# One 105-word row table per hop, a buffer for x, and hop 1's products with a PSUM operand, in a two-hop graph attention kernel

## The reference

```python
edge_index = jnp.stack([src, dst]); head, tail = edge_index
for _ in range(2):
    a_input = jnp.concatenate([ent[head], ent[tail]], axis=-1)
    e_input = jnp.sum((a_input @ fc_w.T + fc_b) * rel[etype], axis=-1)
    e = jax.nn.leaky_relu(e_input, negative_slope=0.2)
    m = jax.ops.segment_max(e, head, num_segments=n)
    exp_e = jnp.exp(e - m[head])
    alpha = exp_e / jax.ops.segment_sum(exp_e, head, num_segments=n)[head]
    ent = jax.ops.segment_sum(ent[tail] * alpha[:, None], head, num_segments=n) + ent
    ent = ent / jnp.maximum(jnp.linalg.norm(ent, axis=-1, keepdims=True), 1e-12)
out = layernorm(x + ent)
```

## Time and profile before

| | us |
|---|---|
| three runs | 2890.5, 2903.3, 2920.0 (median 2903.3) |
| the profiled execution, its own time | 2912.7 |
| its span | 2910.3 |
| VectorE, GpSimd busy | 1850.1, 1780.5 |
| TensorE, ScalarE busy | 1099.4, 860.1 |

### The profile page before, as it was taken

One profiled execution on the slowest core, in us unless ns is written; L12 is line 12 of the kernel. 1 busy time (PEld: TensorE's weight loads), 2 busy tenths in 40 slices (PEclk: granted clock), 3 DMA queues, 4 the chain that ended last, 5 costly groups with the idle time before them and its releaser, 6 DMA issues. The chain is left out here.

```text
span 2910.3 us, 22387 instructions
## 1 busy us (share of the span) xinstructions
PE 1099.4 (38%) x4597; PEld 839.1 (29%) x4597; DVE 1850.1 (64%) x3677; ACT 860.1 (30%) x1608; POOL 1780.5 (61%) x1607
## 2 busy tenths in 40 slices
PE   4688602233233233223322634343433434333310
PEld 4577601122132123222212423221222322222210
DVE  6967863366556556556636567775776668577684
ACT  2334312454455455445521211110111111011121
POOL 1000057277777777777764347777677767767776
PEclk9556555555555555555555556565665656556555
DMA  3455432366676676676664562222222222222110
GB/s 89 124 152 151 137 61 65 61 117 105 117 127 98 115 130 114 103 121 121 100 105 95 69 127 84 67 79 65 79 67 64 81 63 80 65 66 62 55 56 13
DMA packets 235265, 265.66 MB, mean 91 GB/s; under 512 B 182810, under 2 KB 190123, under 8 KB 231636
## 3 DMA queue, kind: packets, MB, share of 16 engines
q1 hardware_dynamic: 184804, 205.51, 32.4%
q0 software_dynamic: 50416, 59.64, 10.3%
HBM read 141.54 MB, written 128.15 MB: 93 GB/s over the span
## 5 line engine op out<-in xcount | busy, mean ns | idle before, releaser
L574 POOL DMA_INDIRECT area<-tail,gi x784 | 805.6, 1028 | 294.1 <-issue 241.3
L574 POOL DMA_INDIRECT area<-head,gi x392 | 465.6, 1188 | 277.2 <-DVE gi L1138 145.2
L623 POOL DMA_INDIRECT out<-area,place x392 | 493.6, 1259 | 119.4 <-issue 119.4
L764 PE MATMUL psR<-area,row_t 128*98 128x512 f16 (+1 forms) x896 | 301.2, 518 | 634.8 <-DVE area L1186 216.4
L672 PE MATMUL psP<-V,vT 65*125 65x40 f32 (+1 forms) x1586 | 317.3, 388 | 170.1 <-issue 65.3
L764 PEld LDWEIGHTS psR<-area,row_t 128*98 128x98 f16 x896 | 157.5, 184 | 772.0 <-issue 535.2
L672 PEld LDWEIGHTS psP<-V,vT 65*125 65x125 f32 (+1 forms) x1586 | 310.0, 304 | 188.2 <-issue 70.2
L664 PE MATMUL psT<-ident,area 128*65 128x128 f32 x393 | 90.1, 420 | 560.5 <-issue 495.4
L664 PEld LDWEIGHTS psT<-ident,area 128*65 128x65 f32 x393 | 80.2, 229 | 569.0 <-issue 569.0
L869 ACT ACTIVATE area<-iota_h,half_hi 128x392 f16<-128x392 f16 x392 | 237.8, 607 | 9.4 <-issue 9.4
L1137 DVE COPY gi<-head_i 128x14 int32 (+1 forms) x28 | 5.0, 180 | 347.1 <-DMA rows<-area 299.4
(11 more groups left out here) (267 smaller groups left out, 2460.0 us busy)
## 6 DMA issues: line engine op xcount, KB each, us to landing
area<-rows SPq DMA_DIRECT2D x28, 1183.0 KB
tail<-area SPq DMA_DIRECT2D x50, 637.5 KB
...
area<-tail,gi POOLq DMA_INDIRECT x784
```

Source lines behind the costliest of these rows:

```text
L574: pool.indirect_dma_start(out=to[:, b, k, 0:tab.shape[1]], out_offset=None, in_=tab, in_offset=bass.IndirectOffsetOnAxis(ap=gi[:, b, n, k: ...
L623: pool.indirect_dma_start(out=out, out_offset=bass.IndirectOffsetOnAxis(ap=place[:, b, k:k + 1].bitcast(U32), axis=0), in_=rowO[:, b, k, 0 ...
L764: last = te.matmul(psR[g % 2][0:HH, 0:w], row_t[:, n, c, :], hot_lo[:, c, 4 * g * P:4 * g * P + w], start=c == 0 and n == 0, stop=c == HB ...
```

## The change

1. One table per hop: `rows0` replaces `tail0` and `head0`, `rows1` replaces the old `rows1` and `tail1`; a row is 105 words (64, one, 20 B, 20 A). Gathers read all 105 words. A chunk's store is one dense DMA of 128 x 1470 words. ScalarE makes a node tile's row with two copies, not four, and SyncE stores it with two DMAs, not four.
2. x in its own place: in hop 0 ScalarE copies the 64 channels of the gathered head rows to `rowX`, a new operation on each chunk right behind `decay`; SyncE stores `rowX` to a new table `head_xs` once that copy is done; VectorE waits before `gi` for the copy (`s_xc` now counts copies), not for the store. In hop 1 SyncE loads 105 words of heads and x by a second DMA.
3. The look-up sums go to a PSUM bank of their own (`psM`) in hop 1. `take_rows` moves from the chunk's start to behind L1369. `hots` waits for the last `choose` (`s_took`), no more for the sums, and TensorE waits for the taken sums just ahead of the sum matmuls. The fourth group's `choose` stands behind `place`.
4. In hop 1 two-tensor products have one operand in PSUM: `ex` and `decay` (ScalarE writes them there), `rd`, `rs`, `mean`, `typ`, iota, the first and last rows' A, A itself, `part`, `first_end`, and the intermediate of `finish` (`via`). Four small copies and a memset at the seam fill what is constant.
5. At the seam GpSimd does one scatter and three gathers where it did two and two.

```diff
-    tail0 = dram("tail0", [N, WT])
-    head0 = dram("head0", [NPAD, WH])
-    tail1 = dram("tail1", [NPAD + N, WT])
-    rows1 = dram("rows1", [NPAD, W1])
+    rows0 = dram("rows0", [NPAD, WE])
+    rows1 = dram("rows1", [NPAD + N, WE])
+    head_xs = dram("head_xs", [NPAD, C])
...
+        rowH = carve(2, K, WE)
+        rowT = carve(2, K, WE)
+        rowO = carve(2, K, WE)
+        rowX = carve(2, K, C)
...
+        held = flatT[:, 0:K * C].rearrange("p (k c) -> p k c", c=C)
+        held_A = flatT[:, 0:K * R].rearrange("p (k r) -> p k r", r=R)
+        held_typ = flatT[:, K * R:2 * K * R].rearrange("p (k r) -> p k r", r=R)
+        held_part = flatT[:, 1024 - CO - 1:1024]
+        small = flatT[:, 1024:1536]
+        held_end, small = small[:, 0:T], small[:, T:]
+        held_rd, held_rs, held_mean, held_iota, held_first, held_last = (
+            small[:, a:a + n] for a, n in ((0, K), (K, K), (2 * K, K), (3 * K, R), (3 * K + R, R), (3 * K + 2 * R, R)))
+        held_ex = psP[:, 1, 512 - 2 * K:512].rearrange("p (n k) -> p n k", n=2)
+        held_decay = psP[:, :, :].rearrange("p n x -> p (n x)")[:, 0:CO * (K + 1)].rearrange("p (c k) -> p c k", k=K + 1)
...
-                for to, of in ((t0, nT), (h0, nH)):
-                    for lo, hi in node_halves:
-                        sp.dma_start(to[lo:hi, cols(j, KN), :], of[lo:hi, b, :, :]).then_inc(s_nst[b], 16)
+                for lo, hi in node_halves:
+                    sp.dma_start(r0v[lo:hi, cols(j, KN), :], nR[lo:hi, b, :, :]).then_inc(s_nst[b], 16)
...
+            def head_x(j, b):
+                sp.wait_ge(s_xc, j + 1)
                 sp.sem_inc(s_turn_sp, 1)
-                sp.dma_start(re[:, cols(j), X0:W1], rowH[:, b, :, 0:C]).then_inc(s_xc[b], 16)
+                sp.dma_start(xe[:, cols(j), :], rowX[:, b, :, :]).then_inc(s_xst[b], 16)
 
             def dump(j, b):
                 sp.wait_ge(s_out, j + 1)
                 sp.sem_inc(s_turn_sp, 1)
-                sp.dma_start(re[:, cols(j), 0:X0], rowO[:, b, :, 0:X0]).then_inc(s_dump[b], 16)
-                sp.dma_start(te[:, cols(j), :], rowO[:, b, :, 0:WT]).then_inc(s_dump[b], 16)
+                sp.dma_start(re[:, cols(j), :], rowO[:, b, :, :]).then_inc(s_dump[b], 16)
...
                     sp.dma_start(rowH[:, b, :, :], re[:, cols(j), :]).then_inc(s_hl[b], 16)
+                    sp.dma_start(rowX[:, b, :, :], xe[:, cols(j), :]).then_inc(s_hl[b], 16)
...
-                    gather(i * 2 + b, b, 0, head0, rowH)
-                    gather(i * 2 + b, b, 1, tail0, rowT)
+                    gather(i * 2 + b, b, 0, rows0, rowH)
+                    gather(i * 2 + b, b, 1, rows0, rowT)
...
+            pool.indirect_dma_start(
+                out=rows1[0:NPAD, :], out_offset=bass.IndirectOffsetOnAxis(ap=seam_i[:, 1:2].bitcast(U32), axis=0),
+                in_=rowO[:, 0, 0, :], in_offset=None, bounds_check=NPAD - 1, oob_is_err=False).then_inc(s_sw, 16)
+            pool.wait_ge(s_sw, 16)
+            for n, of, to, done in ((2, rows1, last_row, s_lr), (3, rows1, seam_row, s_sg), (3, head_xs, seam_x, s_sg)):
...
-                if not (isinstance(j, int) and j == 0):
+                if isinstance(j, int) and 0 < j < 4:
                     pe.wait_ge(s_rank, j)
...
                 pe.wait_ge(s_took, j * 4 + 4)
+                pe.sem_inc(s_turn_pe, 1)
+                if not (isinstance(j, int) and j < 4):
+                    pe.wait_ge(s_rank, j)
                 for k in range(K):
-                    last = te.matmul(psX[:, k:k + 1], chosen[0:HH, k * P:(k + 1) * P], ones[0:HH, 0:1], start=True, stop=True)
+                    last = te.matmul(sums[:, k:k + 1], chosen[0:HH, k * P:(k + 1) * P], ones[0:HH, 0:1], start=True, stop=True)
...
-                for to in (nT, nH):
-                    sc_.copy(to[0:PN, b, :, 0:C], xs[0:PN, b, :, :]).then_inc(s_act, 1)
+                sc_.copy(nR[0:PN, b, :, 0:C], xs[0:PN, b, :, :]).then_inc(s_act, 1)
                 act.wait_ge(s_npr, j + 1)
                 pr = psP[0:PN, :, 0:KN // 2 * 2 * R].rearrange("p n (k r) -> p n k r", r=2 * R)
-                for n, to in ((0, nT[0:PN, b, :, B0:B0 + R].rearrange("p (n k) r -> p n k r", n=2)),
-                              (1, nH[0:PN, b, :, C:WH].rearrange("p (n k) r -> p n k r", n=2))):
-                    sc_.copy(to, pr[:, :, :, n * R:(n + 1) * R]).then_inc(s_nb if n == 1 else s_act, 1)
+                sc_.copy(nR[0:PN, b, :, B0:WE].rearrange("p (n k) r -> p n k r", n=2), pr).then_inc(s_nb, 1)
...
-                    sc_.activation(ex[:, :, :], dl[:, :, :], ACT.Exp).then_inc(s_exp, 1)
+                    ex_, decay_ = (ex[:, :, :], decay) if h == 0 else (held_ex, held_decay)
+                    sc_.activation(ex_, dl[:, :, :], ACT.Exp).then_inc(s_exp, 1)
                     act.wait_ge(s_exp, h * NCH + j + 1)
-                    sc_.copy(decay[:, :, 1:K + 1], ex[:, 0:1, :].to_broadcast([P, CO, K])).then_inc(s_ex, 1)
+                    sc_.copy(decay_[:, :, 1:K + 1], ex_[:, 0:1, :].to_broadcast([P, CO, K])).then_inc(s_ex, 1)
+                    if h == 0:
+                        if not static:
+                            act.wait_ge(s_xst[b], 16 * i)
+                        sc_.copy(rowX[:, b, :, :], rowH[:, b, :, 0:C]).then_inc(s_xc, 1)
...
-                    dve.wait_ge(s_sum, j)
+                    dve.wait_ge(s_took, j * 4)
...
+                via, rd_, rs_, mean_ = (vv, rd, rs, mean) if h == 0 else (held[:, 0:K0, :], held_rd, held_rs, held_mean)
+                link(ve.tensor_tensor(via, agg, wide(rd_[:, 0:K0], K0), ALU.mult))
+                ve.tensor_tensor(vv, via, rowsH[:, :, 0:C], ALU.add).then_inc(s_sq, 1)
...
-                    link(ve.tensor_tensor(vv, vv, wide(rs[:, 0:K0], K0), ALU.mult))
-                    link(ve.tensor_tensor(vv, vv, rowsH[:, :, X0:W1], ALU.add))
+                    link(ve.tensor_tensor(via, vv, wide(rs_[:, 0:K0], K0), ALU.mult))
+                    link(ve.tensor_tensor(vv, via, rowsX, ALU.add))
...
-                    if taking:
-                        take_rows(taking[0])
+                    if taking and h == 0:
+                        take_rows(taking[0], psX)
...
-                        link(ve.tensor_tensor(fa, first_A.unsqueeze(1).to_broadcast([P, K, R]), wide(in_first[:, cc], K, R), ALU.mult))
-                        link(ve.tensor_tensor(la, last_A.unsqueeze(1).to_broadcast([P, K, R]), wide(in_last[:, cc], K, R), ALU.mult))
+                        fa, la = held_A, cap[:, 0:R, :].rearrange("p r k -> p k r")
+                        link(ve.tensor_tensor(fa, held_first.unsqueeze(1).to_broadcast([P, K, R]), wide(in_first[:, cc], K, R), ALU.mult))
+                        link(ve.tensor_tensor(la, held_last.unsqueeze(1).to_broadcast([P, K, R]), wide(in_last[:, cc], K, R), ALU.mult))
                         link(ve.tensor_tensor(fa, fa, la, ALU.add))
...
-                                          ex[:, 1:2, :].to_broadcast([P, CO, K]), ALU.mult))
-                    link(ve.tensor_tensor_scan(S[:, :, :].rearrange("p c k -> p (c k)"), decay[:, :, :].rearrange("p c k -> p (c k)"),
+                                          ex_[:, 1:2, :].to_broadcast([P, CO, K]), ALU.mult))
+                    link(ve.tensor_tensor_scan(S[:, :, :].rearrange("p c k -> p (c k)"), decay_[:, :, :].rearrange("p c k -> p (c k)"),
                                                XI[:, :, :].rearrange("p c k -> p (c k)"), 0.0, ALU.mult, ALU.add))
-                    link(ve.reciprocal(rd[:, :], S[:, C, 1:K + 1]))
+                    link(ve.reciprocal(rd_[:, :], S[:, C, 1:K + 1]))
...
+                        fe = (first_end if h == 0 else held_end)[:, cc]
                         link(ve.tensor_tensor(cap[:, :, :], SM[:, :, 1:K + 1], fe.unsqueeze(1).to_broadcast([P, CO + 1, K]), ALU.mult))
-                        link(ve.tensor_reduce(part[:, :], cap[:, :, :], AX.X, ALU.add))
-                        link(ve.tensor_tensor(first[:, :], first[:, :], part[:, :], ALU.add))
+                        link(ve.tensor_reduce(part_[:, :], cap[:, :, :], AX.X, ALU.add))
+                        link(ve.tensor_tensor(first[:, :], first[:, :], part_[:, :], ALU.add))
                         if nodes:
                             node_squares(j)
+                        if taking and h == 1:
+                            take_rows(taking[0], psM[:, 0:K])
                         if look:
                             choose(look[0], range(2))
...
-                            choose(look[0], range(2, 4))
+                            choose(look[0], range(2, 3 if h == 1 else 4))
 
                     def free():
                         if ahead:
                             if h == 0:
-                                dve.wait_ge(s_xc[b], 16 * (i + 1))
+                                dve.wait_ge(s_xc, j + 1)
...
                         ve.tensor_copy(place[:, b, :], write_f[:, cc]).then_inc(s_row, 1)
+                        if look:
```

(5 more changed lines are left out.)

179 lines of the change are left out of this document (81 added, 98 removed).

## The result

The change made the kernel slower where it was first measured: 3012.9 us median of 4 runs (3003.4 to 3027.9) against 2911.6 us of before, a ratio of 1.036 (1.028 to 1.044). The forecast was 2658 us. On another chip the same program took 2616 us beside 2874 of before (one run each). So there are two questions: what eats the gain here, and why not there. Medians in this document are of fast runs alone, which matters only on chip 9, where three of the changed kernel's ten runs were over 1.5% above its fastest.

A forecast was written before the change was run, and what follows sets the result against it. GpSimd and VectorE, waiting for each other, were taken to bound the kernel. Sort stage -1, hop 0 -85, seam +1 and hop 1 -160 gave -245 us: 2658 us on the median's footing, range 2595 to 2755.

The forecast's parts named there:

- rival A: PE's signals starve while GpSimd never pauses, so hop 0 gets no faster: -160 us, 2743 us; chance 0.15.
- Hop 1, operands, -126 us: Hop 1: with one product operand in PSUM, GpSimd's 135 us of stretched instructions nearly all go, 9 us left: -126 us.
- C: VectorE becomes hop 1's bound, its products with a PSUM operand a quarter slower: -194 us, 2709 us; chance 0.13.
- D: Hop 1's permuted PSUM writes and reads run at a fraction of the rate; doubled, +151 us, 3054 us; chance 0.03.
- Hop 1, look-up, -34 us: Hop 1: sums taken later, 10 us more own work covers most waiting; 34 of GpSimd's 57 us idle go.
- Hop 0, -85 us: Hop 0: index copy no longer waits for x's store; GpSimd is the bound at 40.5 us a chunk: -85 us.
- The 2.2 us a chunk: Hop 0, steady part: what the store of x, awaited before the index copy, costs each chunk.
- The 14.5 us at the start: Hop 0's start: what the store costs there; the indices of chunk 4 come 14.5 us earlier.
- Rival E: The crowd of stores holds PE's signal back in hop 0 and goes with the change: -293 us, 2610 us; chance 0.10.
- B: Hop 1's stretching has another cause than SBUF operands, so hop 1 gains 34 us alone: -119, 2784 us; chance 0.07.
- The seam: Between the hops: a gather more, a scatter less, one ACT copy less, four small VectorE operations more: +1 us.
- The sort stage: Before hop 0: one ACT copy of x less per node tile, but ACT isn't what it waits for: -1 us.

The follow-up runs named there:

- e3d: The changed kernel with hop 1's products back in SBUF, the rest of the change kept, on chip 12: 2827.9 us beside 2936.2 of before.

## Why the prediction was wrong

*The step that failed.* The forecast took PE's signals as prompt in hop 0 ("GpSimd is the bound", -85 us) and as late by a fixed amount in hop 1 ("10 us more of own work in between cover most", -34 us). The runs show an arrival that goes by what GpSimd does: once it issues without pause or stretch, the sums come up to 28 us after PE and VectorE waits 11.0 us a chunk for them. So the two terms came out as +4 and about +220 us of GpSimd's idle time.

*The range.* It ended at 2755, and rival A, whose mechanism is what happened, stood at 2743 with 0.15. A was under-priced in the same way: as "hop 0 gets no faster", with hop 1's -160 kept whole. Hop 1 took 92 us more instead. The prediction had the signs on the table: waits of 50.75 and 28.7 us that ended once GpSimd had run dry, and 121 us of remote waits at L1192. It never asked what lets signals pass in hop 1, where GpSimd hardly runs dry. By e3d it has to do with the stretched DMAs that the change was removing.

*Hop 1, operands, -126 us.* Right: GpSimd's busy time fell by 128.5 us here, and the slowing of VectorE's products that C and D feared is nil (the permuted one, L1369, takes 1757 ns with a PSUM operand and 1778 without on chip 2). The prediction's one row for a stretched write stood beside a scan (L1356 in the earlier trace rows); e3d's L1373 above shows it beside a tensor_tensor. The product L1278, in hop 0 with SBUF operands and in hop 1 with PSUM:

```profile
L1278 DVE TENSOR_TENSOR area<-SM,rd x28: 1664/1678/1682, 430.8 to 1548.7; 128x896 f32<-128x896 f32 x28
...
L1278 DVE TENSOR_TENSOR psT<-SM,psT x28: 1666/1667/1668, 1625.5 to 2565.7; 128x896 f32<-128x896 f32 x28
```

*Hop 1, look-up, -34 us.* Wrong here. "10 us more of own work in between cover most" took the wait of 8.8 us a chunk as a fixed lateness. It was 0 to 14.4 us, and short only as long as the DMAs were stretched; in the changed kernel the sums come up to 28 us late. The wait grew to 11.0 us a chunk, GpSimd's idle time from 57 to 277 us (1279.0 - 762.7 - 239.1).

*Hop 0, -85 us.* Wrong here: +4. GpSimd did run at 38 us a chunk at times, but the stalls of PE's signals gave it back. That was A's mechanism, as far as the timeline shows. On chip 11 the hop did get 83 us shorter, against a slower hop of before, so the size is not the same on all late chips. One reading under this term was also wrong: the 46 us of GpSimd's idle time in 579:1476 are not "mostly one wait of 50.5 us", which ends at 579.45 and so lies almost whole outside the stretch; they are the pauses of 1 to 4 us in its 21 chunks. The 2.2 us a chunk were right all the same. The 14.5 us at the start have no row behind them; the loop's first index copy came 12.6 us earlier (565.6 for 578.2).

*Rival E.* Its cause is refuted: the crowd of stores is gone and ScalarE still waits 47.7 us for PE at L878 on the first chip.

*Where signals are prompt* the sum holds in size: forecast -245, measured 2616.4 - 2874.4 = -258. That is in part luck. The forecast was worked out from a profile with late signals, the kernel before was never profiled without them, and single terms missed in ways that cancel. Hop 1 was to take 1027 us and takes 1002, of which GpSimd is busy 759.6 (756.1 was the floor), 239 are gaps and 4 idle time: the 23 us of idle time and most of the 9 of stretch that I left don't exist. In hop 0 the index copies in the loop run

```profile
L1150 DVEq FUSED_REGOPS  x22: 69/75/75, 514.9 to 1389.8; - x22
```

to 1389.8, forecast 1390, though by other parts: the start is 63 us earlier than 578, not 14.5 (rival E's 50 us, which were a late signal), and a chunk takes 41.7 us and not 40.5. B, C and D are refuted by these runs.

*The seam and the sort stage.* The sort stage is as forecast: hop 0's first gather begins at 378 to 384 us in all profiles, 380 and 383 in those of before. The seam, from hop 0's last gather to hop 1's first, was to take 1 us more than 82. It takes 77 us here and 60 on chip 2; why it is shorter there was not followed up.
